# Reordered opening and turn, and idle TensorE instructions that fix where each visit stands in an instruction page

## The chip, the cores and the metric

The kernel runs on one core of one Trainium2 chip, as one launch. The metric is the device time of that core in microseconds (us), lower is better. TensorE multiplies matrices, VectorE (DVE), ScalarE (ACT) and GpSimd (POOL) do the rest of the arithmetic, SyncE (SP) issues transfers. Each engine has a sequencer that reads its own instruction stream in program order; engines wait for each other on semaphores.

## The reference, cut to what matters

Four attention modules follow each other. The change is in the first, L0, which has two cross-attention layers with 16 heads of width 128 over 32 sequences of 64 tokens, model width 256:

```python
def _cross_attention(q_in, kv_in, wq, bq, wk, bk, wv, bv, wo, bo, bias_k, bias_v):
    qh = (q_in @ wq + bq).reshape(b, q_len, H, K)      # H=16, K=128
    kh = (kv_in @ wk + bk).reshape(b, t, H, K)
    vh = (kv_in @ wv + bv).reshape(b, t, H, K)
    kh = concatenate([kh, bias_k]); vh = concatenate([vh, bias_v])
    weights = softmax(einsum('bqhk,bthk->bhqt', qh, kh) / sqrt(K))
    return einsum('bhqt,bthk->bqhk', weights, vh).reshape(b, q_len, H * K) @ wo + bo

x = x + _cross_attention(layer_norm(x), ctx, ...)       # layer 1
x = x + _cross_attention(layer_norm(x), ctx, ...)       # layer 2
x = x + gelu(layer_norm(x) @ w_fc1 + b_fc1) @ w_fc2 + b_fc2
```

After it come a perceiver attention, a decoder layer and a non-local block on the same data (the stretch from about 930 us on), which the change doesn't touch.

## The kernel before, in words

The 2,048 tokens are cut into 4 chunks (`NCH`) of 512 tokens. Heads are taken two at a time (a pair, with its own 1 MB pack of weights), so each layer has 8 pairs x 4 chunks = 32 steps `t`, and both layers together 64. Each of a step's products in float32 precision is three float32r matmuls (`split3`: high x high, high x low, low x high), all recorded at line 174.

TensorE's order is written out by hand. A block `d` handles the steps a = 2d and b = 2d+1. In an ordinary block (`pe_block`) TensorE does, in this order:

1. `pe_upper`: in every second pair of blocks first eight value tiles of the two steps before (`pe_values_behind`, 6 matmuls of 128x512 each); then four keys (`pe_key`, 6 matmuls of 128x512 each: two heads of a, two of b); two outputs (`pe_out`, 24 matmuls of 128x256 each); two transposes of probabilities.
2. `pe_queries`: four queries, 6 matmuls of 128x512 each.
3. `pe_visit`: probabilities times values of two earlier steps (`pe_heads`, L873, 128 records of matmuls and 128 of weight loads) and then the scores of a and b (`pe_scores`, L774, 64 and 64 records). A visit is 384 TensorE instructions, all tiny.

Four stretches are written separately: the opening (`pe_block_first`, `pe_block_second`: steps 0 to 3, with the layer norm of all chunks), the turn between the layers (`pe_block_turn`, `pe_block_after`: d = 16 and 17, with the layer norm of layer 2), the single steps at the end (`pe_singles`, steps 60 to 63), and the warm-up (16 matmuls on zeros, L1134, that wait for a memset). DVE, ACT and POOL have hand-written orders to match: `dve_attend`, `dve_block_turn`, `dve_block_after`, `act_attend`, `pool_attend`. Of these matter here: `dve_shift` (L1343, L1346: subtract the row's maximum from the scores; the next keys wait for it, since they reuse the scores' PSUM banks), `dve_values` (L1379, L1380: copy values out of PSUM), `context_dve` (L388: low part of the context), `norm0.dve_x` (L585: normalised rows), `norm0.dve_lo` (L602: low part of the normed rows, which queries wait for).

## Time and profile before

| | |
|---|---|
| median of 3 runs | 1558.56 us (1557.78 to 1559.69) |
| the profiled execution's own time | 1559.04 us |
| its span, first to last instruction | 1557.3 us |
| PE busy | 1505.2 us (97%) |
| DVE / ACT / POOL busy | 62% / 56% / 27% |
| mean granted TensorE clock | 0.993 |

The sum in the prediction is made against the profiled execution, 1559.04 us, which lies 0.5 us over the median. PE is matmuls, PEld weight loads, which overlap with matmuls. Waits are named by the instruction that ended last; "issue" means that the engine waited for nothing that the profile shows.

### The profile page before, as it was taken

What the parts mean: (1) busy time and instruction counts of PE and PEld (TensorE: products, weight loads), DVE (VectorE), ACT (ScalarE), POOL (GpSimd) and SP (SyncE); (2) the same over time, 40 slices, a digit from 0 to 9 for tenths busy, and PEclk for the clock granted to TensorE, in tenths of its full rate; (3) what the DMA queues carried; (4) which work ended last, traced back from release to release, by engine and by line L of the source; (5) the groups of instructions that cost most, each with busy time, mean ns of one, the idle gap of its engine ahead of it and who ended that gap; (6) DMA issues with size and microseconds to landing.
All of it is one profiled execution on the core that took longest, in us unless ns stands there. A gap on an engine that the chain in (4) does not pass through costs nothing. (4 is left out here: it accounts for less than half of the span.)

```text
span 1557.3 us, 41338 instructions
## 1 busy us (share of the span) xinstructions
PE 1505.2 (97%) x17264; PEld 1305.5 (84%) x17264; DVE 973.1 (62%) x2135; ACT 866.4 (56%) x1626; POOL 413.4 (27%) x445
## 2 busy tenths in 40 slices
PE   8899999999999999999999999999999999999996
PEld 7688888888888788888888888988878888888864
DVE  7746546554566664555646676479996558865366
ACT  5454353354455554454453466577777567775476
POOL 1320120210201510210210123036774206542052
PEclk9999999999999999999999999999999999999998
DMA  6010010010010010010010000020002000000001
GB/s 214 1 69 2 29 42 1 29 43 1 29 42 1 29 42 2 29 42 2 29 43 29 29 2 28 1 83 2 3 29 82 1 29 3 30 2 28 8 22 55
DMA packets 17832, 46.20 MB, mean 30 GB/s; under 512 B 1360, under 2 KB 11616, under 8 KB 14704
## 3 DMA queue, kind: packets, MB, share of 16 engines
q1 hardware_dynamic: 13456, 39.33, 7.3%
q10 hardware_dynamic: 4192, 4.24, 0.8%
q8 instruction: 137, 2.24, 0.6%
q14 instruction: 47, 0.39, 0.1%
HBM read 39.37 MB, written 4.19 MB: 28 GB/s over the span
## 5 line engine op out<-in xcount | busy, mean ns | idle before, releaser
L174 PE MATMUL ps<-ch,W 128*128 128x512 f32 (+1 forms) x2484 | 582.9, 384 | 12.7 <-DVE arena L1346 6.0
L174 PEld LDWEIGHTS ps<-ch,W 128*128 128x128 f32 x2484 | 437.8, 189 | 98.3 <-issue 5.9
L174 PEld LDWEIGHTS ps<-W,split_arena 128*128 128x128 f32 x3084 | 388.4, 188 | 23.5 <-issue 4.7
L174 PE MATMUL ps<-W,split_arena 128*128 128x256 f32 x3084 | 401.9, 283 | 3.4 <-DVE split_arena L1678 2.6
L1343 DVE TENSOR_REDUCE small<-ps 128x4 f32<-128x260 f32 x128 | 53.9, 421 | 241.3 <-PE ps L774 241.1
L1184 ACT ACTIVATE arena<-ps,hbias 128x512 f32<-128x512 f32 x128 | 87.9, 688 | 206.6 <-PE ps L174 205.6
L174 PE MATMUL ps<-W,ch 128*128 128x512 f32 (+1 forms) x864 | 193.7, 381 | 0.3
L1169 ACT ACTIVATE arena<-ps 64x256 f32<-64x256 f32 x256 | 96.8, 378 | 170.2 <-PE ps L860 166.4
L174 PEld LDWEIGHTS ps<-W,ch 128*128 128x128 f32 x864 | 154.6, 188 | 31.8 <-ACT arena L2166 0.9
L1678 DVE TENSOR_TENSOR split_arena<-arena,split_arena 128x512 fp32r<-128x512 f32 x96 | 72.1, 751 | 124.8 <-ACT split_arena L1710 115.0
L1370 DVE TENSOR_TENSOR x_sb<-ps,x_sb 128x512 f32<-128x512 f32 x128 | 87.0, 689 | 97.4 <-PE ps L174 97.2
L2440 POOL TENSOR_TENSOR arena<-arena,small 128x1024 f32<-128x1024 f32 x48 | 95.0, 1980 | 126.7 <-DVE small L2299 126.7
L1707 ACT ACTIVATE arena<-ps,cols 128x512 f32<-128x512 f32 x96 | 65.9, 687 | 92.5 <-PE ps L174 92.4
L219 POOL COPY hbias<-raw 128x8 f32<-128x8 f32 x15 | 3.3, 220 | 413.9 <-PE ps L174 413.9
L1191 ACT ACTIVATE arena<-ps,hbias 128x512 f32<-128x512 f32 x128 | 84.6, 686 | 35.9 <-PE ps L174 35.0
L1336 DVE SCALAR_TENSOR_TENSOR split_arena<-ps,hbias,split_arena 128x256 fp32r<-128x256 f32 x256 | 104.5, 475 | 0.0
L1176 ACT ACTIVATE split_arena<-ps,hbias 128x512 fp32r<-128x512 f32 x128 | 77.7, 687 | 14.0 <-PE ps L873 14.0
L613 POOL TENSOR_TENSOR small<-small 128x4 f32<-128x4 f32 x24 | 27.5, 1148 | 186.5 <-DVE small L486 172.7
L774 PE MATMUL ps<-arena 128*64 128x65 f32 x2048 | 69.7, 224 | 6.0 <-issue 5.9
L873 PEld LDWEIGHTS ps<-arena 64*64 64x64 f32 x4096 | 62.9, 135 | 13.2 <-issue 11.1
L1197 ACT ACTIVATE arena<-arena 128x260 f32<-128x260 f32 x128 | 52.4, 423 | 37.0 <-DVE arena L1346 37.0
L774 PEld LDWEIGHTS ps<-arena 128*64 128x64 f32 x2048 | 63.8, 138 | 10.1 <-issue 7.9
(172 smaller groups left out, 2020.4 us busy)
## 6 DMA issues: line engine op xcount, KB each, us to landing
raw<-wpack SPq DMA_DIRECT2D x23, 1028.0 KB, 4.8
rows<-vb_in SPq DMA_DIRECT2D x8, 512.0 KB, 5.7
x_sb<-x_in SPq DMA_DIRECT2D x4, 512.0 KB, 9.7
arena<-ctxT SPq DMA_DIRECT2D x4, 512.0 KB, 9.9
spill<-x_sb ACTq DMA_DIRECT2D x1, 2048.0 KB, 11.3
arena<-spill ACTq DMA_DIRECT2D x1, 2048.0 KB, 8.3
arena<-ctx_tok SPq DMA_DIRECT2D x16, 128.0 KB, 2.0
out<-x_sb SPq DMA_DIRECT2D x7, 256.0 KB, 2.5
```

Source lines behind the costliest of these rows:

```text
L174: last = e.matmul(dst, lhs[a], rhs[b], start=start and n == 0, stop=stop and n == 2, skip_group_check=True)
L774: ins = e.matmul(ps[r:r + SEQ, scores_bank(t) + h, n // 2 * KEYS0:(n // 2 + 1) * KEYS0], qs[t % 2][h][:, n * SEQ:(n + 1) * SEQ], ks[t % 2] ...
L873: ins = e.matmul(ps[dims, heads_bank(t) + b, at:at + SEQ], values[keys, h * DH0 + d * SEQ:h * DH0 + (d + 1) * SEQ], pts[t % 2][h][keys, n, ...
L1169: ins = e.activation(pts[t % 2][h][b * SEQ:(b + 1) * SEQ], own[:, :, b * SEQ:(b + 1) * SEQ], ACT.Copy)
L1176: e.activation(head_split(t, h, 0), head_cells(t, h), ACT.Identity, bias=head_col(t, 3, h)).then_inc(a_oh, 1)
L1184: e.activation(ks[u % 2][h][:, :, key_slots(h)], cut(ps[:, keys_bank(u) + h, :], BPC), ACT.Identity, bias=head_col(u, 1, h)).then_inc(a_ke, 1)
L1191: e.activation(qs[u % 2][h], ps[:, query_bank(u) + h, :], ACT.Identity, bias=head_col(u, 0, h)).then_inc(a_qe, 1)
L1336: ins = e.scalar_tensor_tensor(head_split(t, h, 1)[:, :, b, :], head_cells(t, h)[:, :, b, :], head_col(t, 3, h), head_split(t, h, 0)[:, :, ...
L1370: e.tensor_tensor(xs, cut(ps[:, b + j, :], 2), xs, ALU.add).then_inc(a_acc, 1)
L1678: e.tensor_tensor(gsp[f % 2][1], gelu[:, f % 2, :], gsp[f % 2][0].bitcast(F32), ALU.subtract).then_inc(s["gl"].sem, 1)
L1707: e.activation(gelu[:, f % 2, :], ps[:, f % 2, :], func, bias=col(f"fb{which}", f)).then_inc(s["gel"].sem, 1)
L2440: e.tensor_tensor(cells, cells, many(inv[w % 2], nk), ALU.mult).then_inc(nrm_done, 1)
```

## The change

It has four parts.

1. A new helper `idle(e, n)` puts n instructions on TensorE that only wait, for a semaphore (`none_ok`) that has been set since the first microseconds: 106 before the warm-up; 10 after each value tile of `pe_values_behind`; 24 after each key of a block whose number is a multiple of 4 (d = 4, 8, 12, 16, 20, 24, 28); 14 after six of the value tiles in `pe_block_after`. Four blocks then hold 2 x 80 + 96 = 256 of them.
2. Waits are moved out of the visits, onto earlier instructions (queries, outputs), so that a visit holds none.
3. Opening: low parts of context chunks 2 and 3 go from DVE to POOL (`context_lo`), the normalised rows of chunks 1 to 3 from DVE to ACT (`act_tiles`), and norms stand elsewhere in TensorE's order.
4. Turn and single steps: norms, value copies, low parts and POOL's powers are reordered; two PSUM bank choices follow.

```diff
@@ -548,7 +548,7 @@
             def act_tiles(self, e, c, l):
 
                 g = l * NCH + c
-                e.wait_ge(second_mean, c + 1)
+                e.wait_ge(second_mean, l * NCH + c)
                 e.wait_ge(self.s["T"].sem, self.s["T"].at(g * KT - 1))
                 for j in range(TPC):
                     ins = e.activation(xn[:, j, :], x_sb[:, c * TPC + j, :], ACT.Identity, scale=rstd[:, j:j + 1],
...
@@ -877,28 +876,38 @@
 
         none = sm[1].rearrange("p n k -> p (n k)")[:, 0:P]
 
+        PAGE_START, PAGE_TURN = 106, 14
+
+        def idle(e, n):
+
+            for _ in range(2 * n):
+                e.wait_ge(none_ok, 1)
+
         def pe_values_behind(e, d):
 
             a, b = 2 * d, 2 * d + 1
             for i in range(2):
                 e.wait_ge(a_sub, two(a, i))
                 pe_values(e, a, i)
+                idle(e, 10)
             for i in range(2):
                 e.wait_ge(a_sub, two(b, i))
                 pe_values(e, a, 2 + i)
+                idle(e, 10)
             e.wait_ge(a_ol, two(a - 2, 1))
             for i in range(2):
                 pe_values(e, b, i)
+                idle(e, 10)
             e.wait_ge(a_ol, two(b - 2, 1))
             for i in range(2):
                 pe_values(e, b, 2 + i)
+                idle(e, 10)
 
         def pe_visit(e, d):
 
             a, b = 2 * d, 2 * d + 1
             e.wait_ge(a_qe, two(a, 1))
             pe_heads(e, a - 2)
-            wait(e, a_acc, two(b - 4, 1))
             pe_heads(e, b - 2)
             pe_scores(e, a)
             pe_scores(e, b)
@@ -906,28 +915,32 @@
         def pe_upper(e, d):
 
             a, b = 2 * d, 2 * d + 1
-            behind = values_behind(d - 1)
-            if behind:
+            if values_behind(d - 1):
                 pe_values_behind(e, d - 1)
-            for h in range(2):
-                if behind:
+                for h in range(2):
                     e.wait_ge(a_ve, values_done(a - 2, h))
-                e.wait_ge(a_sub, two(a - 2, h))
-                pe_key(e, a, h)
-            for h in range(2):
-                if behind:
+                    pe_key(e, a, h)
+                for h in range(2):
                     e.wait_ge(a_ve, values_done(b - 2, h))
+                    pe_key(e, b, h)
+                pe_out(e, a - 4)
+                e.wait_ge(a_ve, values_done(b - 2, TPC - 1))
+                pe_out(e, b - 4, a)
+            else:
+                some = 24 if d % 4 == 0 else 0
+                for h in range(2):
+                    e.wait_ge(a_sub, two(a - 2, h))
+                    pe_key(e, a, h)
+                    idle(e, some)
                 e.wait_ge(a_ol, two(a - 4, 1))
-                pe_key(e, b, h)
-            if behind:
-                e.wait_ge(a_ve, values_done(a - 2, TPC - 1))
-            e.wait_ge(a_sub, two(b - 2, 1))
-            pe_out(e, a - 4)
-            if behind:
-                e.wait_ge(a_ve, values_done(b - 2, TPC - 1))
-            pe_out(e, b - 4)
+                for h in range(2):
+                    pe_key(e, b, h)
+                    idle(e, some)
+                e.wait_ge(a_sub, two(b - 2, 1))
+                pe_out(e, a - 4)
+                e.wait_ge(a_ol, two(b - 4, 1))
+                pe_out(e, b - 4, a)
             for i in range(2):
-                e.wait_ge(a_ke, two(a, i))
                 pe_transpose(e, a - 2 + i)
 
         def pe_queries(e, d):
...
@@ -960,19 +978,20 @@
             for h in range(2):
                 e.wait_ge(a_qe, two(0, h))
                 pe_key(e, 1, h)
-            e.wait_ge(a_ve, values_done(0, TPC - 1))
-            pe_norm(e, 0, 1)
             norm_out(e, 0, 0)
             for i in range(2):
                 pe_values(e, 1, i)
+            e.wait_ge(a_ve, values_done(0, TPC - 1))
+            pe_norm(e, 0, 1)
             for i in range(2):
                 e.wait_ge(a_ke, two(0, i))
                 pe_values(e, 1, 2 + i)
+            norm_out(e, 0, 1)
+            for h in range(2):
+                pe_query(e, 1, h)
             e.wait_ge(a_ke, two(1, 1))
             pe_norm(e, 0, 2)
-            norm_out(e, 0, 1)
-            for h in range(2):
-                pe_query(e, 1, h)
+            e.wait_ge(a_kb, 1)
             e.wait_ge(a_ve, values_done(1, TPC - 1))
             pe_scores(e, 0)
             pe_scores(e, 1)
...
@@ -1040,28 +1061,35 @@
             for i in range(2):
                 e.wait_ge(a_ke, two(b, i))
                 pe_values(e, a, i)
+                idle(e, PAGE_TURN)
             e.wait_ge(a_acc, two(a - 4, 1))
             for i in range(2):
                 pe_values(e, a, 2 + i)
+                idle(e, PAGE_TURN)
             e.wait_ge(a_pt, two(b - 2, 1))
             pe_norm(e, 1, 2)
             e.wait_ge(a_acc, two(b - 4, 1))
             pe_heads(e, a - 2)
             norm_out(e, 1, 2)
             pe_heads(e, b - 2)
-            for i in range(TPC):
+            for i in range(2):
                 e.wait_ge(a_ve, values_done(a, i))
                 pe_values(e, b, i)
+                idle(e, PAGE_TURN)
+            e.wait_ge(a_ve, values_done(a, TPC - 1))
+            pe_norm(e, 1, 3)
             e.wait_ge(a_ol, two(a - 2, 1))
-            pe_norm(e, 1, 3)
+            for i in range(2):
+                pe_values(e, b, 2 + i)
             for h in range(2):
                 e.wait_ge(a_ve, values_done(b, h))
                 pe_query(e, a, h)
-            for h in range(2):
-                e.wait_ge(a_ve, values_done(b, 2 + h))
+            norm_out(e, 1, 3)
+            for h in range(2):
                 pe_query(e, b, h)
             e.wait_ge(a_ol, two(b - 2, 1))
             pe_scores(e, a)
+            e.wait_ge(a_ve, values_done(b, TPC - 1))
             pe_scores(e, b)
 
         def pe_singles(e):
...
@@ -1143,18 +1184,21 @@
                     pe_block(e, d)
             pe_singles(e)
             next0.lead(e)
+            e.wait_ge(a_ol, two(STEPS - 2, 1))
             pe_out(e, STEPS - 2)
...
@@ -1233,16 +1277,19 @@
             act_keys(e, 0)
             act_norm(e, 0, 0)
             context_act(e, 1)
+            first_act(e, 4)
             act_queries(e, 0)
-            first_act(e, 4)
+            context_act(e, 2)
+            norm0.act_tiles(e, 1, 0)
             act_keys(e, 1)
             act_norm(e, 0, 1)
-            context_act(e, 2)
-            act_norm(e, 0, 2)
+            norm0.act_tiles(e, 2, 0)
             context_act(e, 3)
             act_queries(e, 1)
+            act_norm(e, 0, 2)
 
             act_exp(e, 0)
+            norm0.act_tiles(e, 3, 0)
             act_keys(e, 2)
             act_exp(e, 1)
...
@@ -1466,16 +1514,17 @@
             dve_mean(e, 1, 3)
             dve_values(e, a, (2, 3))
             dve_heads(e, a - 2)
+            dve_values(e, b, (0, 1))
             norm0.dve_lo(e, 2, 1)
+            norm0.dve_lo(e, 3, 1)
             dve_heads(e, b - 2)
-            dve_values(e, b)
-            norm0.dve_lo(e, 3, 1)
+            dve_values(e, b, (2, 3))
 
         def dve_attend(e):
             e.memset(minus_half, -0.5).then_inc(s_small.sem, 1)
             e.memset(none, 0.0).then_inc(none_ok, 1)
             dve_stats(e, 0, 0)
-            context_dve(e, 0)
+            context_lo(e, 0)
             first_dve(e, 0)
             norm0.dve_newton(e, 0)
             e.scalar_tensor_tensor(nmean, mv[:, :, 0], -1.0, rstd, ALU.mult, ALU.mult).then_inc(first_mean, 1)
@@ -1486,24 +1535,24 @@
                 first_dve(e, i)
             norm0.dve_lo(e, 0)
 
+            dve_values(e, 0, (0, 1))
+            context_lo(e, 1)
+            dve_stats(e, 0, 1)
+            dve_values(e, 0, (2, 3))
+            dve_mean(e, 0, 1)
             dve_bias_keys(e, 0)
-            dve_stats(e, 0, 1)
-            dve_values(e, 0)
-            context_dve(e, 1)
-            norm0.dve_x(e, 1)
             first_dve(e, 4)
             dve_stats(e, 0, 2)
+            dve_values(e, 1, (0,))
+            dve_mean(e, 0, 2)
             norm0.dve_lo(e, 1)
-            norm0.dve_x(e, 2)
-            dve_values(e, 1)
-            context_dve(e, 2)
+            dve_values(e, 1, (1, 2, 3))
             dve_stats(e, 0, 3)
+
+            dve_shifts(e, 0)
+            dve_mean(e, 0, 3)
+            dve_shifts(e, 1)
             norm0.dve_lo(e, 2)
-            norm0.dve_x(e, 3)
-            context_dve(e, 3)
-
-            dve_shifts(e, 0)
-            dve_shifts(e, 1)
             dve_scale(e, 0)
             dve_scale(e, 1)
             norm0.dve_lo(e, 3)
...
@@ -1570,7 +1619,10 @@
             e.tensor_copy(hbias[0], raw[:, PACK:PCOLS]).then_inc(hb_ok, 1)
             pair_bias(e, 0)
             norm0.pool_pow(e, 1)
+            e.wait_ge(c_lo.sem, c_lo.at(KT + KT - 1))
+            context_lo(e, 2)
             norm0.pool_pow(e, 2)
+            context_lo(e, 3)
             norm0.pool_pow(e, 3)
             e.wait_ge(s_raw, 16)
             pair_columns(e, 1)
@@ -1583,8 +1635,11 @@
                 split_pool(e, n, n - 2)
                 if n % 2:
                     split_half(e, n)
-            for c in range(NCH):
-                norm0.pool(e, c, row("bo2"), 1)
+            for c in (0, 2):
+                norm0.pool_pow(e, c, 1)
+                norm0.pool_pow(e, c + 1, 1)
+                norm0.pool_row(e, c, row("bo2"), 1)
+                norm0.pool_row(e, c + 1, row("bo2"), 1)
             for n in range(NHP + 1, 2 * NHP + 1):
                 split_pool(e, n, n - 2)
                 if n % 2 and n < NPAIR - 1:
```

The instructions that only wait are not listed in the orders below.

TensorE in the opening, from the first four value tiles to the first scores; before:

```order
L174 MATMUL ps<-W,ch 128x512 x24
L174 MATMUL ps<-ch,W 128x512 x24
L627 MATMUL ps<-cols,norm_arena 128x128 x8
L174 MATMUL ps<-W,ch 128x512 x24
L627 MATMUL ps<-cols,norm_arena 128x128 x8
L174 MATMUL ps<-ch,W 128x512 x12
L774 MATMUL ps<-arena 64x65 x32
```

and of the change:

```order
L174 MATMUL ps<-W,ch 128x512 x24
L174 MATMUL ps<-ch,W 128x512 x24
L174 MATMUL ps<-W,ch 128x512 x12
L627 MATMUL ps<-cols,norm_arena 128x128 x8
L174 MATMUL ps<-W,ch 128x512 x12
L174 MATMUL ps<-ch,W 128x512 x12
L627 MATMUL ps<-cols,norm_arena 128x128 x8
L773 MATMUL ps<-arena 64x65 x32
```

The two norms (L627, transposes) moved behind 12 more matmuls each; the scores stay last.

DVE just ahead of the first scores' maximum (L1343 before, L1390 now); before:

```order
L602 TENSOR_TENSOR ch<-norm_arena,ch 128x512 [waits n_hi] x2
L508 TENSOR_TENSOR small<-small 128x4 [waits n_pow,n_var]
L510 TENSOR_TENSOR small<-small 128x4 [waits n_r1]
L512 TENSOR_SCALAR small<-small 128x4 [waits n_r2]
L514 TENSOR_TENSOR small<-small 128x4 [waits n_r3]
L585 TENSOR_SCALAR norm_arena<-x_sb,small 128x256 [waits n_r4,n_T]
L585 TENSOR_SCALAR norm_arena<-x_sb,small 128x256 x3
L388 TENSOR_TENSOR ch<-arena,ch 128x512 [waits c_hi] x2
L1343 TENSOR_REDUCE small<-ps 128x4 [waits a_scores]
```

and of the change:

```order
L1426 TENSOR_TENSOR arena<-ps,arena 128x256 [waits a_values]
L1427 TENSOR_TENSOR arena<-ps,arena 128x256
L448 BN_STATS small<-x_sb 128x6 [waits s_x3,n_x]
L448 BN_STATS small<-x_sb 128x6 x3
L472 BN_AGGR small<-small 128x2 [waits n_st]
L472 BN_AGGR small<-small 128x2 x3
L486 TENSOR_SCALAR small<-small 128x4 [waits n_ag]
L1390 TENSOR_REDUCE small<-ps 128x4 [waits a_scores]
```

The low parts of chunk 2 (L602), the Newton steps and rows of chunk 3 (L508 to L585) and the context's low part (L388) no longer stand ahead of it; only copies of values and the statistics of chunk 3 do.

TensorE in `pe_block_after` (d = 17), from the norm of chunk 2 to the scores; before:

```order
L627 MATMUL ps<-cols,norm_arena 128x128 x8
L873 MATMUL ps<-arena 64x64 x64
L174 MATMUL ps<-W,ch 128x512 x24
L627 MATMUL ps<-cols,norm_arena 128x128 x8
L174 MATMUL ps<-ch,W 128x512 x24
L774 MATMUL ps<-arena 64x65 x32
```

and of the change:

```order
L627 MATMUL ps<-cols,norm_arena 128x128 x8
L872 MATMUL ps<-arena 64x64 x64
L174 MATMUL ps<-W,ch 128x512 x12
L627 MATMUL ps<-cols,norm_arena 128x128 x8
L174 MATMUL ps<-W,ch 128x512 x12
L174 MATMUL ps<-ch,W 128x512 x24
L773 MATMUL ps<-arena 64x65 x32
```

The norm of chunk 3 (second L627) now stands between the value tiles of step b, not behind them.

## Rows read from the trace of the kernel before

**Rows 1.** The page's head: the span, busy time of each engine, instruction fetches.

```profile
span 1557.3 us, 41338 instructions
PE 1505.2 (97%) x17264; PEld 1305.5 (84%) x17264; DVE 973.1 (62%) x2135; ACT 866.4 (56%) x1626; POOL 413.4 (27%) x445
...
q8 instruction: 137, 2.24, 0.6%
```

**Rows 2.** Waits of TensorE, 0 to 930 us: us in total, times, longest.

```profile
PE ps L174 <- DVE arena L1346: 6.0, 2, 5.5
PE ps L774 <- issue: 5.9, 9, 1.8
PE ps L174 <- DVE arena L1380: 3.1, 2, 1.6
...
PE ps L627 <- DVE arena L1380: 2.2, 1, 2.2
PE ps L174 <- DVE ch L602: 1.7, 2, 0.9
```

**Rows 3.** TensorE in order of time, two visits: start, us, work, [idle before].

```profile
92.98 2.09 PE L873 MATMUL ps<-arena 64*64 64x64 f32 x128
95.01 2.08 PE L774 MATMUL ps<-arena 128*64 128x65 f32 x64
97.02 5.79 PE L174 MATMUL ps<-ch,W 128*128 128x512 f32 x24
...
114.85 2.09 PE L873 MATMUL ps<-arena 64*64 64x64 f32 x128
...
118.97 0.81 PE L774 MATMUL ps<-arena 128*64 128x65 f32 x20 [0.58 <-issue]
119.71 5.79 PE L174 MATMUL ps<-ch,W 128*128 128x512 f32 x24
```

**Rows 4.** The last visit with such a stop, same columns.

```profile
766.87 2.09 PE L873 MATMUL ps<-arena 64*64 64x64 f32 x128
...
771.47 2.81 PE L174 MATMUL ps<-ch,W 128*128 128x512 f32 x11
```

**Rows 5.** Waiting instructions by line: duration ns min/median/max, first to last start us.

```profile
L864 PEldq EVENT_SEMAPHORE  x1: 51/51/51, 56.5 to 56.5; - x1
L865 PEldq EVENT_SEMAPHORE  x1: 2263/2263/2263, 56.6 to 56.6; - x1
L865 PEldq EVENT_SEMAPHORE  x1: 51/51/51, 110.7 to 110.7; - x1
L2755 DVEq EVENT_SEMAPHORE  x13: 21/21/21, 0.8 to 1.9; - x13
...
L2755 PEldq EVENT_SEMAPHORE  x3: 51/51/51, 0.8 to 1.1; - x3
```

**Rows 6.** TensorE in order of time, the opening.

```profile
2.28 5.69 PE L1134 MATMUL ps<-arena 128*128 128x128 f32 x32 [2.28 <-DVE arena L1476]
8.27 1.20 PE L811 MATMUL ps<-ch,W 128*128 128x512 f32 x4 [0.29 <-ACT W L276]
...
43.77 7.32 PE L174 MATMUL ps<-ch,W 128*128 128x512 f32 x24 [5.46 <-DVE arena L1346]
...
59.33 2.10 PE L873 MATMUL ps<-arena 64*64 64x64 f32 x128
...
64.30 11.22 PE L174 MATMUL ps<-W,ch 128*128 128x512 f32 x48
```

**Rows 7.** TensorE in order of time, the turn.

```profile
476.42 1.22 PE L627 MATMUL ps<-cols,norm_arena 128*128 128x128 f32 x8 [2.18 <-DVE arena L1380]
477.29 7.29 PE L174 MATMUL ps<-ch,W 128*128 128x512 f32 x24
...
517.86 3.01 PE L174 MATMUL ps<-ch,W 128*128 128x512 f32 x12 [1.60 <-DVE arena L1380]
521.76 3.00 PE L174 MATMUL ps<-ch,W 128*128 128x512 f32 x12 [0.89 <-DVE ch L602]
```

100 lines of the change are left out of this document (61 added, 39 removed).

## The prediction, on record before the changed kernel ran

> **What bounds the kernel now.** I read the page first, then the waits of TensorE, then its timeline. TensorE (PE) is busy 97% of the span and no other engine passes 62% [rows 1], so a microsecond counts only where PE stops. Up to 930 us, the stage that is changed, its stops are few [rows 2]: the first scores' shift (L1346, 5.5 us at once), value copies (L1380), low parts (L602), and nine stops of 5.9 us together inside the scores (L774) that end by "issue": no engine is late.
>
> Those nine come at a fixed place. An undisturbed visit lasts from 92.98 to 97.02, 4.04 us; the visit at 114.85 lasts until 119.71, 4.86 us, and PE stands still after 44 of its 64 scores records [rows 3]. The stream holds 34,528 weight loads and matmuls [rows 1] and 705 waiting instructions, and is fetched in 137 pieces [rows 1]: 257 each, so I take a page as 256. Counting the built program from the stop in the visit at 59.33 to that at 118.97 gives 1,256 loads and matmuls plus 24 waits, 1,280 = 5 pages; every other stop also lies a whole number of pages away. In instructions from a visit's first one to the next page start, the visits that stop stand at 45 to 134 (45, 68, 86, 93, 118, 134), the others at 3, 20, 38, 163, 183, 205 and more. So a stop needs two page starts inside, or just at the end of, one visit's 384 quick instructions: the second page isn't there yet. The last such visit takes 4.60 us [rows 4], the first 4.97 [rows 6]; eleven visits are over 4.04 us by 9.2 us in all (first 0.93, last 0.56).
>
> The skill is cited once on this: the Trainium skill, "Runtime: NRT & Kernel Launch", section on instruction fetch mechanics, has blocks of 256 instructions, as counted here, but says that crossing a boundary is mostly hidden. The trace disagrees for visits (0.58 us [rows 3]); by that rule the new places would give back nothing and the sum below would be 8.1 us higher.
>
> **The change part by part.**
>
> *Places of the visits: -8.1 us.* Counted in the built program, the distances to the next page start become 14, 14, 14, 190, repeating, both in the safe sets. So 9.2 us go. New risks: the visit in the turn stands at 137 and a single-step visit at 59 with its second page start 7 instructions before the end. I book the turn's below and 1.1 us for the single one, between the smallest stop I see and the longest, 1.8 [rows 2].
>
> *What an idle instruction costs: 0.11 us of PE's sequencer.* The trace shows no long run of them on PE, so this is bounded. Its record lasts 51 ns [rows 5]: the lower end. Two adjacent ones, L864 and L865, start at 56.5 and 56.6 [rows 5], 0.1 us apart; a run of three on PE, which also set a semaphore, starts 0.8 to 1.1, 0.15 apart: the upper end. That a run costs start to start, not by its records, is shown on DVE: 13 with 21 ns records take from 0.8 to 1.9, 0.09 each. I take 0.11, nearest to the pair.
>
> *What covers it.* The sequencer runs ahead of the engine. The wait ahead of the visit (L865) is done at 110.7 and the visit starts at 114.85 [rows 3, 5]: 4.15 us at 0.234 us a matmul (11.22/48 [rows 6]) is about 18 matmuls, 35 instructions. At the end of a visit these 35 are scores, 2.01 us for 128 instructions [rows 3], only 0.55 us of work.
>
> *24 after each key, seven blocks: +32.9 us.* A key is 6 matmuls, 1.41 us. The keys come straight after a visit. When the first key's 12 instructions are issued, 23 scores instructions (0.36 us) and the key (1.41) are ahead: 1.77 us. 24 idles take 2.64 us, so PE stops about 0.9 us (0.05 to start again). Now nothing is ahead: after each of the other three keys it stops 2.64 - 1.41 + 0.03 = 1.26 us. That is 0.92 + 3 x 1.26 = 4.7 us a block, and d = 4, 8, 12, 16, 20, 24, 28 make 32.9. Behind the idles stand outputs, transposes and queries; no other engine gives the time back, because PE has no stops of theirs to spare there. What PE does later in the block (outputs, so DVE's additions) is late by as much.
>
> The Trainium skill ("TensorE: Matmul & The Clock Gate", facts table) gives the engine's queue 64 places; the trace shows 35. By 64 the first stop of each block would shrink by at most 29 scores instructions, 0.46 us, and the sum by 3.2 us.
>
> *10 after each value tile: 0.* 1.1 us against 1.41 us of matmuls; the cover grows with each. Without cover it would still be free. *14 in the block after the turn: +0.* 1.54 against 1.41, 0.13 short each, which the 0.55 us or more ahead covers.
>
> *106 at the start: +11.3 us.* The first one waits for the memset, as the warm-up does now (2.28 [rows 6]). 106 x 0.11 = 11.7, so the warm-up runs from 13.9 and, at 5.7 us, ends at 19.6; the first keys start at 8.27 now. The loads and first splits that they wait for are then long done.
>
> *Opening, given back: -9.3, new waits +0.5.* With PE 11.3 us late and DVE not, what PE waited for is there: 5.46 at the first keys of block 1, and with it the slow clock behind it (24 matmuls in 7.32 us [rows 6] against 5.79 [rows 3]: 1.5), 1.5 of L1380 (3.1 less the turn's 1.6 [rows 2, 7]), 0.8 of L602 (1.7 - 0.9). The reordering helps too: between scores and shift DVE has only copies and one set of statistics left. POOL gets two low parts and three powers in line; a power behind them can hold a norm, hence the 0.5. Opening together: 11.3 - 9.3 + 0.5 = +2.5.
>
> *Turn: -3.3 us.* The norm of chunk 1 waits 2.18 us for the sixth value copy [rows 7]. The low part that stood among the copies still stands there, but statistics and Newton steps now overlap POOL's power: 0.8 less. Of the slow clock behind it (7.29 against 5.79) I count half, 0.8. In the block after, queries waited 1.60 and 0.89 [rows 7] for copies and a low part that now come earlier; the norm that is pulled forward may wait 0.6 for ACT's rows: -1.9. A visit there gains a page stop of 0.5 and another loses 0.3: +0.2.
>
> Single steps: waits change places, 0 +-1. Later stages: same code, other places in the page, and none of their stops shows this pattern, 0 +-1.
>
> **Sum.** 1559.0 + 32.9 (24s) + 2.5 (opening) - 3.3 (turn) - 8.1 (pages) = **1583.0 us** for a profiled execution, and 1582.6 against the median; I say 1583.
>
> **The rivals.**
>
> *Idles cost their record, 51 ns; the kernel gets faster.* For it: the record. Against it: rows 5, where no engine starts the next waiting instruction when the record of the last ends. Then 24 take 1.22 us, under the key's 1.41, and nothing stops. The start costs 5.4 instead of 11.7, so keys start 5.1 us later and, being less late, still wait 1.5 us of the 9.3: 5.1 - 9.3 + 1.5 = -2.7. 1559.0 - 2.7 - 3.3 - 8.1 = 1545. It turns at about 0.075 us an idle: then three stops of 0.42 and one of 0.1 in seven blocks make 9.5 us and the start costs 8. Chance 0.11, and 0.02 for landing on the turning point (within 0.2% of before, which is about what a measurement tells from no change).
>
> *The clock falls in the 24s.* PE then works 1.41 and rests 1.26 us, four times. It fell to 1.2 GHz (granted 0.5) after 2.18 us of rest in the turn, not after the 1.8 us stop [rows 2, 7]; each fall costs 1.5 us (7.29 against 5.79). One fall in each of seven blocks: 1583 + 10.5 = 1593. Chance 0.12.
>
> *Places don't matter:* something else in the visits stops PE and the 9.2 us stay: 1591. Against it, the whole pages between stops. Chance 0.05.
>
> *Idles at 0.15,* as in the run of three: 24 take 3.6, a block stops 0.96 more four times, seven blocks 27, the start 4: 1583 + 31 = 1614. They also set a semaphore there, the new ones don't. Chance 0.04.
>
> The forecast itself has 0.66.
>
> **How the numbers follow.** 1583 is the forecast's; its own range is 1573 to 1592: 0.01 us on an idle moves it 8 us (24 x 4 x 7 x 0.01 and the start), opening and turn 3 each. The range for 8 in 10 takes in the clock and the places: 1566 to 1598; outside lie the faster rival, 0.15 and a little more. Faster 0.11, same 0.02, slower 0.87.
>
> **What would show it.** In the changed profile: the first keys at about 19.6 us; in blocks 4, 8, ... four stops by "issue" ahead of L174, one near 0.9 and three near 1.26 us; waiting instructions 0.11 us apart; all ordinary visits 4.04 us, no issue stop in the scores save one in the single steps; no 5 us stop at 40 us; the norm in the turn waiting 1.4 us or less. It is wrong if idles lie 0.05 to 0.07 us apart, for then the 24s vanish under the keys, or if a stopped PE loses its clock each time.

## The result and the profile after

The changed kernel takes 1591.76 us (median of 4 runs, 1589.39 to 1592.99) against 1559.12 us (1557.78 to 1560.3) for the kernel before beside it: ratio 1.0205, 95% interval 1.0189 to 1.0221. The forecast was 1583, its range 1566 to 1598. The profiled execution of the change took 1591.85 us, 32.8 more than that of before; its span is 32.8 us longer too. Below, a "stop" is a stretch in which PE stands still between two matmuls, and "the 24s" are the 24 idle instructions behind each key.

The head of the page, which answers to [rows 1]:

```profile
span 1590.1 us, 42905 instructions
...
PE 1509.6 (95%) x17264; PEld 1302.6 (82%) x17264; DVE 972.4 (61%) x2122; ACT 874.3 (55%) x1638; POOL 419.1 (26%) x449
...
q8 instruction: 143, 2.34, 0.6%
```

PE does the same 17,264 matmuls in nearly the same busy time (4 us more); nearly all of the loss is standing still. The waits of PE up to 930 us, us in total, times, longest, which answer to [rows 2]:

```profile
PE ps L174 <- issue: 19.1, 21, 1.2
PE ps L1175 <- issue: 13.7, 1, 13.7
PE ps L174 <- DVE split_arena L1383: 7.8, 7, 1.2
PE ps L627 <- DVE arena L1427: 3.0, 1, 3.0
PE ps L627 <- ACT norm_arena L554: 2.0, 1, 2.0
PE ps L773 <- issue: 1.3, 3, 0.7
```

L174 has 21 + 7 = 28 stops: four in each of the seven blocks with 24 idles. (Those put down to L1383 are such stops too; block 4 below has one.) The 5.5 us stop of before [rows 2] is gone and a 13.7 us one stands at the start; the page stops in the scores went from nine to three.

PE in order of time, in four stretches: opening, visit and block 4, turn, block behind the turn (start, us, work, [idle before]). It answers to [rows 3, 6, 7].

```profile
13.72 6.66 PE L1175 MATMUL ps<-arena 128*128 128x128 f32 x32 [13.72 <-issue]
20.14 1.17 PE L811 MATMUL ps<-ch,W 128*128 128x512 f32 x4
...
49.70 5.75 PE L174 MATMUL ps<-ch,W 128*128 128x512 f32 x24
...
63.64 2.10 PE L872 MATMUL ps<-arena 64*64 64x64 f32 x128
...
66.80 1.85 PE L773 MATMUL ps<-arena 128*64 128x65 f32 x56 [0.69 <-issue]
68.58 1.67 PE L174 MATMUL ps<-W,ch 128*128 128x512 f32 x6
...
119.18 2.10 PE L872 MATMUL ps<-arena 64*64 64x64 f32 x128
...
123.22 1.67 PE L174 MATMUL ps<-ch,W 128*128 128x512 f32 x6
125.58 1.61 PE L174 MATMUL ps<-ch,W 128*128 128x512 f32 x6 [0.69 <-issue]
128.18 1.60 PE L174 MATMUL ps<-ch,W 128*128 128x512 f32 x6 [0.99 <-DVE split_arena L1383]
130.95 1.63 PE L174 MATMUL ps<-ch,W 128*128 128x512 f32 x6 [1.17 <-issue]
133.60 6.00 PE L174 MATMUL ps<-W,split_arena 128*128 128x256 f32 x48 [1.02 <-issue]
...
497.60 1.97 PE L627 MATMUL ps<-cols,norm_arena 128*128 128x128 f32 x8 [3.01 <-DVE arena L1427]
...
535.94 1.06 PE L627 MATMUL ps<-cols,norm_arena 128*128 128x128 f32 x8 [1.99 <-ACT norm_arena L554]
```

- The first keys start at 20.14 (8.27 before [rows 6]). From 68.58 on the ordinary blocks run; before, they began at 64.30 [rows 6]: +4.3 us, with the first visit as long as before, 4.94 us here.
- The visit at 119.18 ends at 123.22: 4.04 us, no stop. Of 28 full visits 26 are so, where before it was 17; only the first (63.64) and the last, at 875.75 (4.60 us), are longer.
- Block 4 stops four times: once by 0.69 and then by about 1 us of idle time. From start to start, less a key's 1.41, the four are 0.95, 1.19, 1.36 and 1.24 us, where 0.92 and three of 1.26 were forecast. From the visit ahead of it to the next (at 145.86) it takes 26.68 us; such a block without idles takes 21.87. That is 4.8 us a block and 33.8 in seven.
- In the turn the norm waits 3.01 us, not 2.18 [rows 7], and another norm waits 1.99. From the visit ahead of the turn (461.39) to the first ordinary one behind (566.25) it is 104.86 us, 4.83 of them the idles; before it was 98.66 (445.85 to 544.51): +1.4.

The idles themselves, those of the start, of which 105 are recorded: duration ns min/median/max, first to last start in us:

```profile
L884 PEldq EVENT_SEMAPHORE  x105: 51/51/51, 2.3 to 13.5; - x105
```

Start to start that is 11.2/104 = 0.108 us, with records of 51 ns. The first idle behind the first key of block 4 starts at 122.89, 0.33 us ahead of that key (123.22); the forecast had 0.36, from a sequencer 35 instructions ahead.

Where 32.7 us went, from the starts of the last visit (923.83 before, 956.52 after), in the forecast's own terms:

| term | forecast | measured |
|---|---|---|
| 24 idles, seven blocks | +32.9 | +33.8 |
| opening to the first ordinary block | +2.5 | +4.3 |
| turn | -3.3 | +1.4 |
| visits' places, with the single steps and the rest | -8.1 | -7.6 + 0.8 |
| sum | +24.0 | +32.7 |

Of the 0.8, 0.25 lies in the single steps (75.92 us from the end of the last full visit to the start of the last visit before, 76.17 after). The other 0.6 lies in blocks behind visits that no longer stop: before, such a block was up to 0.18 us shorter than 17.83, so a part of the stop came back.

So the one large term held, and two of the terms I built on waits, opening and turn, did not; the turn has the wrong sign. The experiments take the terms one at a time.

### The profile page after: what moved, and what is told of

Its sections match the earlier page's. It is cut to its first block and busy times, and to the rows that moved or that the text cites. A ratio compares the mean times of both kernels' runs of the same rounds, so it can differ in the third digit from the quotient of the medians.

```text
span 1590.1 us, 42905 instructions
## 1 busy us (share of the span) xinstructions
PE 1509.6 (95%) x17264; PEld 1302.6 (82%) x17264; DVE 972.4 (61%) x2122; ACT 874.3 (55%) x1638; POOL 419.1 (26%) x449
## 5 line engine op out<-in xcount | busy, mean ns | idle before, releaser
L174 PE MATMUL ps<-ch,W 128*128 128x512 f32 (+1 forms) x2484 | 585.9, 384 | 22.9 <-issue 11.8
L174 PEld LDWEIGHTS ps<-ch,W 128*128 128x128 f32 x2484 | 434.6, 188 | 114.8 <-issue 32.2
L174 PEld LDWEIGHTS ps<-W,split_arena 128*128 128x128 f32 x3084 | 388.0, 188 | 32.4 <-issue 14.7
L174 PE MATMUL ps<-W,split_arena 128*128 128x256 f32 x3084 | 402.3, 283 | 10.7 <-issue 7.6
L1390 DVE TENSOR_REDUCE small<-ps 128x4 f32<-128x260 f32 x128 | 53.8, 420 | 234.2 <-PE ps L773 234.1
L174 PE MATMUL ps<-W,ch 128*128 128x512 f32 (+1 forms) x864 | 194.2, 382 | 0.3
L174 PEld LDWEIGHTS ps<-W,ch 128*128 128x128 f32 x864 | 154.4, 188 | 31.8 <-ACT arena L2221 0.9
L1383 DVE SCALAR_TENSOR_TENSOR split_arena<-ps,hbias,split_arena 128x256 fp32r<-128x256 f32 x256 | 104.4, 474 | 0.0
L1220 ACT ACTIVATE split_arena<-ps,hbias 128x512 fp32r<-128x512 f32 x128 | 78.0, 688 | 13.2 <-PE ps L872 13.0
L872 PEld LDWEIGHTS ps<-arena 64*64 64x64 f32 x4096 | 63.1, 135 | 13.2 <-issue 11.6
L2378 DVE TENSOR_REDUCE small<-ps 128x8 f32<-128x1024 f32 (+1 forms) x48 | 58.4, 1217 | 18.4 <-PE ps L2124 18.0
L872 PE MATMUL ps<-arena 64*64 64x64 f32 x4096 | 68.0, 220 | 1.3 <-ACT arena L1235 0.8
L773 PE MATMUL ps<-arena 128*64 128x65 f32 x2048 | 67.9, 223 | 1.3 <-issue 1.3
```

The lines of the kernel that those rows point to most:

```text
L174: last = e.matmul(dst, lhs[a], rhs[b], start=start and n == 0, stop=stop and n == 2, skip_group_check=True)
L773: ins = e.matmul(ps[r:r + SEQ, scores_bank(t) + h, n // 2 * KEYS0:(n // 2 + 1) * KEYS0], qs[t % 2][h][:, n * SEQ:(n + 1) * SEQ], ks[t % 2] ...
L872: ins = e.matmul(ps[dims, heads_bank(t) + b, at:at + SEQ], values[keys, h * DH0 + d * SEQ:h * DH0 + (d + 1) * SEQ], pts[t % 2][h][keys, n, ...
L1220: e.activation(head_split(t, h, 0), head_cells(t, h), ACT.Identity, bias=head_col(t, 3, h)).then_inc(a_oh, 1)
L1383: ins = e.scalar_tensor_tensor(head_split(t, h, 1)[:, :, b, :], head_cells(t, h)[:, :, b, :], head_col(t, 3, h), head_split(t, h, 0)[:, :, ...
```

## The experiments

Times are medians, and the ratio is to the kernel before on the same chip, with its 95% interval. Differences between versions are of medians, which came from different chips in part; the kernel before lay between 1559.1 and 1559.7 us on them. "The turn" is the time from the start of the visit ahead of it to that of the first ordinary visit behind it; "over 4.04" is what the 28 full visits take above 4.04 us each.

### Without the 24s

```diff
-                some = 24 if d % 4 == 0 else 0
+                some = 0
```

> The changed kernel without the 24 idles after each key (7 blocks, 672 instructions less); the other idles stay. Theory A (an idle costs TensorE's sequencer 0.11 us and the 24s outlast the key ahead of them): 7 x 4.83 us go, but the visits no longer stand at one place; counted in the program, nine visits stand at 46 to 118 from the next page start and one at 126, which by the stops of the kernel before is 8.6 us; 1591.8 - 33.8 + 8.6 - 0.9 = 1565.7. Rival B (the loss comes from the waits that were moved out of the visits and the idles are free): about 1592 plus page stops, 1600.

Measured: 1565.31 us, 1.0036 (1.0024 to 1.0048), as theory A has it. The 24s cost 26.5 us net: 33.8 from the stops, less what the places give, since without them the visits drift through the page and are 9.9 us over 4.04 again.

### No idle at all, the order of the change

```diff
-            for _ in range(2 * n):
-                e.wait_ge(none_ok, 1)
+            return
```

> The changed kernel with every idle left out: the reordered opening and turn alone. Theory A: 24s gone (-33.8), page stops come back (six visits at 120, four at 44, two at 124: +12), and the start is 11.9 us earlier of which the opening's own waits take back 5 to 8: 1591.8 - 33.8 + 12 - 5.5 = about 1564. The opening ends (start of the third block) between 61 and 65 us against 64.3 before and 68.6 in the changed kernel. Rival B: 1590 or more.

Measured: 1558.06 us, 0.9991 (0.9982 to 1.0). I expected 1564, with the ordinary blocks from 61 to 65 us. The ordinary blocks start at 56.56 us, where before it was 64.30 [rows 6]: the new order of the opening alone gives 7.7 us, and TensorE was not late at all in this run (first keys at 7.90). The visits are 13.2 over 4.04, the turn takes 100.6.

### The kernel before with only the 24s

```diff
                 pe_key(e, a, h)
+                idle(e, 24 if d % 4 == 0 else 0)
```

> The kernel before with the 24 idles after each key of blocks 4, 8, ... 28 and nothing else of the change. Theory A: +33.8, and page stops change from 9.2 to about 5.6 us since the visits move: 1559.1 + 33.8 - 3.6 = 1589.3, with four stops in each of seven blocks. Rival B (idles free): 1556.

Measured: 1593.19 us, 1.0210 (1.0194 to 1.0225), 4 us over the expectation. The 24s cost about the same in the old order: the keys of block 4, with their stops, take 10.3 us (119.52 to 129.84) and 10.4 in the change (123.22 to 133.60). What I missed is the visits, which at their shifted places were 9.6 over 4.04, not 5.6. A stop at a given distance comes back, but not with the same length (0.1 to 1.7 us in this run).

### The same idles, spread

The four blocks keep 256 idles, but never more than 8 in one spot outside `pe_values_behind` (10) and the block behind the turn (14): behind keys, behind each half of the outputs, behind queries, and in the turn behind value tiles in place of queries. The edit in part:

```diff
-                some = 24 if d % 4 == 0 else 0
+                some = 8 if d % 4 == 0 else 0
...
+                    idle(e, some // 2)
```

> The changed kernel with the same 96 idles in each of the seven blocks, at most 8 in one place: 8 after each of four keys, 4 after each quarter of the two outputs, 8 after each of four queries (in the turn: four value tiles). Every visit stands at the same place in its page as in the changed kernel. Theory A (an idle is free while its run is shorter than the matmuls ahead of it: 0.88 against 1.41 us, 0.44 against 0.72): 1591.8 - 33.8 = 1558.0, and no stop in those blocks. Rival C (each idle costs time wherever it stands): no change, 1592.

Measured: 1558.26 us, 0.9991 (0.9982 to 1.0). The same number of idles costs nothing when none of the runs outlasts the work in front of it: 33.5 us lie between this kernel and the change. Block 4 in it, PE in order of time:

```profile
122.88 5.79 PE L174 MATMUL ps<-ch,W 128*128 128x512 f32 x24
128.50 5.92 PE L174 MATMUL ps<-W,split_arena 128*128 128x256 f32 x48
```

The 24 matmuls of the keys run through in 5.6 us, which took 10.4 with the 24s.

### Runs of seven lengths

```diff
-                some = 24 if d % 4 == 0 else 0
+                some = {4: 12, 8: 14, 12: 16, 16: 18, 20: 20, 24: 22, 28: 28}.get(d, 0)
```

> The change with 12, 14, 16, 18, 20, 22 and 28 idles behind each key in blocks 4, 8, 12, 16, 20, 24 and 28, in place of 24 in each. It measures the price of an idle inside the kernel. My theory, 0.11 us an idle and hidden up to the 1.41 us of a key: no stop at 12, nearly none at 14 (0.1 or less each), and per block about 1.1, 2.0, 2.9, 3.8 and 6.5 us for 16, 18, 20, 22 and 28 idles. Rival (a fixed price for any run of idles, such as a restart of the queue): the blocks with 12 and 14 stop too, and 28 costs hardly more than 16. The visits leave their common place, so some of them stop in a page again.

Measured: 1581.72 us, 1.0141 (1.0126 to 1.0157). From the end of a visit to the start of the next a block without idles takes 17.83 us; with four runs of 12, 14, 16, 20, 22 and 28 idles it took 0, 0.3, 1.2, 2.8, 3.7 and 6.3 us more (block 16 is the turn and is left out). I had expected 1.1, 2.9, 3.8 and 6.5 for the last four. From 20 to 28 that is 3.5 us for 32 idles, 0.11 each; the price starts between 12 and 14, where 0.11 x 13 equals a key's 1.41. No fixed price shows. Keys of block 28 in it (28 idles each):

```profile
814.14 1.63 PE L174 MATMUL ps<-ch,W 128*128 128x512 f32 x6 [1.08 <-DVE arena L1393]
817.21 1.63 PE L174 MATMUL ps<-ch,W 128*128 128x512 f32 x6 [1.44 <-issue]
820.25 1.63 PE L174 MATMUL ps<-ch,W 128*128 128x512 f32 x6 [1.42 <-issue]
```

From 814.14 to 817.21 are 3.07 us, 28 x 0.11: the key lies wholly beneath its idles.

### The kernel before with only the 106 at the start

```diff
         def pe_attend(e):
+            for _ in range(2 * 106):
+                e.wait_ge(none_ok, 1)
             e.wait_ge(none_ok, 1)
```

> The kernel before with only the 106 idles at the start. My theory: the warm-up and the first keys come 11.9 us later (first keys at 20.1 us), the stops that follow in the old opening (5.5 at the first keys of block 1 with its slow clock, copies and low parts, 9.3 us together) are given back because the other engines are not late, so block 2 starts 2.6 us later than before, at about 66.9 us; the visits stand at other places, of which some 9 again stop, so they give nothing. Together 1561 to 1563 us. Rival (the other engines' work is itself tied to TensorE, so the stops are not given back): block 2 starts 8 to 12 us later, 1567 to 1571 us.

Measured: 1568.07 us, 1.0063 (1.0049 to 1.0077). My theory fell here: the ordinary blocks start at 74.27 us, 10.0 later than before, as the rival has it. The stop that I had "given back" stands where it was. PE in order of time, then DVE:

```profile
18.75 1.17 PE L811 MATMUL ps<-ch,W 128*128 128x512 f32 x4
...
53.31 7.83 PE L174 MATMUL ps<-ch,W 128*128 128x512 f32 x24 [5.45 <-DVE arena L1348]
```

```profile
37.95 1.29 DVE L602 TENSOR_TENSOR ch<-norm_arena,ch 128x512 fp32r<-128x512 f32 x2 [0.49 <-ACT ch L651]
...
47.27 1.29 DVE L602 TENSOR_TENSOR ch<-norm_arena,ch 128x512 fp32r<-128x512 f32 x2
...
49.87 1.38 DVE L585 TENSOR_SCALAR norm_arena<-x_sb,small 128x256 f32<-128x256 f32 x4 [0.18 <-DVE small L514]
51.17 1.28 DVE L388 TENSOR_TENSOR ch<-arena,ch 128x512 fp32r<-128x512 f32 x2
52.37 0.42 DVE L1345 TENSOR_REDUCE small<-ps 128x4 f32<-128x260 f32 x1
```

The stop is 5.45 us long, against 5.46 [rows 6], although PE is 10.5 us late (18.75 against 8.27). DVE reaches the maximum (L1345) only after low parts, value copies, statistics, Newton steps, rows and a context part, almost back to back from 37.95 on (0.7 us of waits in 14.4). The first of these (L602, 37.95) itself waited for ACT's high part (L651), which is made of PE's transposes. In the kernel before the same DVE operation starts at 28.40, 9.55 us earlier: DVE had moved back with PE.

### The start's 106 idles spread over the opening

On top of the spread version: 5 or 6 idles behind each of the 21 groups of 6 matmuls in the two opening blocks, none before the warm-up. All visits from the first full one on keep their places. The edit in part:

```diff
+        opening = iter([PAGE_START // groups + (n < PAGE_START % groups) for n in range(groups)])
+        def few(e):
+            idle(e, next(opening, 0))
...
+                few(e)
...
-            idle(e, PAGE_START)
```

> The change with its 256 idles a four-block spread (at most 8 in one place), and now also the 106 idles of the start taken from before the warm-up and laid 5 at a time behind the groups of 6 matmuls of the two opening blocks, so that each run hides under 1.4 us of matmuls. All visits stand at the same places of a page as with the 106 at the start. My theory (an idle costs 0.11 us of TensorE's sequencer and is free under cover; the 106 pay 11.7 us before any work is there): the start of block 2 comes at 56.6 to 57.5 us instead of 67.9, and the kernel takes about 1547 us. Rival (the reordered opening is bound by DVE and ACT, so that the early start only moves the wait): start of block 2 at 61 or later and 1551 to 1553 us.

Measured: 1546.37 us, 0.9917 (0.9904 to 0.9931), 11.9 us faster than with the 106 in front. PE in order of time:

```profile
8.80 1.17 PE L811 MATMUL ps<-ch,W 128*128 128x512 f32 x4
...
38.37 5.75 PE L174 MATMUL ps<-ch,W 128*128 128x512 f32 x24
...
57.24 3.01 PE L174 MATMUL ps<-W,ch 128*128 128x512 f32 x12
```

There is no 5.5 us stop behind the scores although the first keys start at 8.80: the order removes it, lateness does not. The ordinary blocks start at 57.24, 10.7 us earlier than with the 106 in front (67.89). Another 1.5 us is in the turn (98.5 against 100.05), where the granted clock fell to 0.5 in the profiled execution of the spread version (behind a stop of 2.90 us) and stayed at 1.00 in this one (behind 2.87). That is in part luck of the execution: the mean clock of the eleven runs of the spread version, one kernel, lies between 0.993 and 0.997.

### POOL's order in the turn as before

```diff
-            for c in (0, 2):
-                norm0.pool_pow(e, c, 1)
-                norm0.pool_pow(e, c + 1, 1)
-                norm0.pool_row(e, c, row("bo2"), 1)
-                norm0.pool_row(e, c + 1, row("bo2"), 1)
+            for c in range(NCH):
+                norm0.pool(e, c, row("bo2"), 1)
```

On top of the spread version. The reason for it is in the trace of the change: DVE (two stretches) and then POOL, in order of time:

```profile
485.46 0.16 DVE L514 TENSOR_TENSOR small<-small 128x4 f32<-128x4 f32 x1
...
491.41 0.62 DVE L508 TENSOR_TENSOR small<-small 128x4 f32<-128x4 f32 x1
492.06 0.66 DVE L510 TENSOR_TENSOR small<-small 128x4 f32<-128x4 f32 x1
492.76 0.67 DVE L512 TENSOR_SCALAR small<-small 128x4 f32<-128x4 f32 x1
493.46 0.65 DVE L514 TENSOR_TENSOR small<-small 128x4 f32<-128x4 f32 x1
494.15 0.16 DVE L1439 SCALAR_TENSOR_TENSOR small<-small 128x4 f32<-128x4 f32 x1
```

```profile
490.29 1.01 POOL L613 TENSOR_TENSOR small<-small 128x4 f32<-128x4 f32 x1 [5.93 <-DVE small L486]
491.27 2.83 POOL L409 TENSOR_TENSOR x_sb<-x_sb,rows 128x256 f32<-128x256 f32 x4
```

While POOL adds rows (491.27 to 494.10), each of DVE's four Newton steps takes 0.62 to 0.67 us; at 485.46, without POOL beside it, a step of the same shape takes 0.16, and so does L1439 just after the rows. With POOL's powers put ahead of the rows, DVE gets the power early and meets the rows.

> The change with spread idles, and POOL's order in the turn as it was before (for each chunk first its powers, then its row additions) in place of powers of two chunks and then rows of two chunks. My theory (the turn lost because POOL's row additions now run while DVE does its Newton steps on 128x4, which take 0.62 to 0.70 us instead of 0.16 and delay value copies and rows of chunk 3): DVE's Newton steps come back to about 0.16 us, the turn from visit 15 to visit 19 takes 97 to 98.5 us instead of 100.05, and the kernel 1555 to 1557 us. Rival (the loss comes from TensorE's own new order in the turn): the Newton steps get shorter and the turn stays at 100.

Measured: 1553.24 us, 0.9963 (0.995 to 0.9977), 5.0 us faster than with the change's POOL order. The same step of DVE, then PE's norm, in this run:

```profile
473.12 0.16 DVE L514 TENSOR_TENSOR small<-small 128x4 f32<-128x4 f32 x1
```

```profile
476.76 1.09 PE L627 MATMUL ps<-cols,norm_arena 128*128 128x128 f32 x8 [1.44 <-DVE arena L1433]
...
513.14 1.06 PE L627 MATMUL ps<-cols,norm_arena 128*128 128x128 f32 x8 [0.92 <-ACT norm_arena L554]
```

The turn takes 95.39 us, better than the 97 to 98.5 I gave: both norms wait less (1.44 and 0.92 against 2.90 and 1.6 in the spread version), and the granted clock doesn't fall behind the first.

### The kernel before with the change's POOL order

The reverse edit, in the kernel before:

```diff
-            for c in range(NCH):
-                norm0.pool(e, c, row("bo2"), 1)
+            for c in (0, 2):
+                norm0.pool_pow(e, c, 1)
...
+                norm0.pool_row(e, c + 1, row("bo2"), 1)
```

> The kernel before with one edit: POOL's order in the turn as in the change (powers of chunks 0 and 1, then the row additions of both; the same for 2 and 3). My theory (the row additions, 0.75 us each, hold up VectorE's small operations with two operands in SBUF): VectorE's Newton steps of chunk 1 take 0.6 to 0.7 us instead of 0.16, the stop of 2.18 us at the norm in the turn grows to 4 to 4.5 us, chunk 3 loses less, and the kernel is 2 to 4.5 us slower, 1561.5 to 1564 us. Rival (POOL's order only hurts in TensorE's new order): within 1 us of before.

Measured: 1563.96 us, 1.0021 (1.0012 to 1.0030), so some 3.3 us slower (4.6 by the medians), by the ratio within the 2 to 4.5 expected; the stop at the norm grew to 3.62 us, less than the 4 to 4.5 expected. DVE, then PE, in order of time:

```profile
471.78 0.66 DVE L510 TENSOR_TENSOR small<-small 128x4 f32<-128x4 f32 x1
```

```profile
477.95 1.97 PE L627 MATMUL ps<-cols,norm_arena 128*128 128x128 f32 x8 [3.62 <-DVE arena L1380]
```

The slow Newton steps appear here too, in the old order of TensorE and DVE; the turn takes 102.8 us instead of 98.66. POOL's order is the cause in both.

### Both remedies

The edits of the last two versions of the change in one kernel:

```diff
-            idle(e, PAGE_START)
...
+                few(e)
...
+            for c in range(NCH):
+                norm0.pool(e, c, row("bo2"), 1)
```

> The two edits that helped, together: the idles of the start spread over the opening blocks and POOL's order in the turn as before, with the spread 256 idles a four-block. If they are independent (one acts before 57 us, the other in the turn), the turn from visit 15 to visit 19 takes 95.4 us and the kernel 1546.4 - 4.9 = 1541.5 us (1540.5 to 1542.5). Rival (the turn's gain depends on where the opening left the other engines or on transfers that come at another moment): 1543 or more.

Measured: 1542.83 us, 0.9891 (0.9875 to 0.9906). The turn takes 95.0. The median lies 1.3 us over the expected sum and just under the rival's 1543; the profiled execution took 1541.48, so the runs don't decide between the two. One thing would make the sum too large: the 1.5 us that the first edit's profile gained in the turn, by the kept clock, are in the second edit's gain too.

### Other places

On top of both remedies:

```diff
-        PAGE_START, PAGE_TURN = 106, 14
+        PAGE_START, PAGE_TURN = 136, 14
...
-                some = 8 if d % 4 == 0 else 0
+                some = 8 if d % 4 == 0 and d != TURN or d == TURN + 1 else 0
```

> As the version with both edits, but 136 instead of 106 idles in the opening and 64 of the turn block's idles moved to the block behind it, so that the visits stand 240 or 160 instructions before the next page start instead of 14 or 190, and the turn's visit at 171. My theory (a stop needs the second page start inside a visit with the sequencer's lead used up; at 14 it comes 112 instructions before the visit's end and is marginal: stops of 0.3 to 0.6 us remained in 5 visits and 0.9 in the first; at 240 and 160 only one page start lies inside the visit's quick part and is preceded by slow instructions): no stop in any ordinary visit but small ones, the sum over 4.04 us falls from 3.1 to under 0.7 us, and the kernel is 2 to 3 us faster than the version with both edits alone, 1538.5 to 1540 us. Rival (14 was as good as any place and the remaining stops come from transfers that delay the fetch): same time within 1 us.

Measured: 1542.45 us, 0.989 (0.9873 to 0.9906): the same, as the rival has it. My theory was right only on the visits. All full visits but the first take 4.04 us, so 240 and 160 are cleaner places than 14; but in the version with both remedies the visits behind the first, at 14 and 190, were only 1.0 over. The first visit stops more, by 1.30 us and among its heads, behind 242 instructions, where the first page start stands at 243, and the block behind the turn, where the 64 idles went, takes 0.9 more. The first visit's stop:

```profile
52.61 2.02 PE L874 MATMUL ps<-arena 64*64 64x64 f32 x121
55.93 0.34 PE L874 MATMUL ps<-arena 64*64 64x64 f32 x7 [1.30 <-issue]
```

### The reordering alone, with POOL's old order

The version without any idle, and:

```diff
+            for c in range(NCH):
+                norm0.pool(e, c, row("bo2"), 1)
```

> No idle instruction at all, the reordered opening, turn and single steps, and POOL's order in the turn as before: what the reordering alone gives without the visits' places. The version without idles took 1558.06; with POOL's order the turn gives 4.7 back, so 1553.4 us (1552.5 to 1554.5); visits stop at their unplanned places by 10 to 13 us in total. Against the version with both edits the difference, about 12 us, is what places are worth. Rival: places worth only 9 us, the stops of the kernel before; then 1550.5.

Measured: 1553.13 us, 0.9954 (0.994 to 0.9968). Its visits are 14.0 over 4.04; in the version with both remedies it was 1.9. The places are worth 10.3 us in time (12.1 in the visits' own lengths). PE's waits, first row:

```profile
PE ps L773 <- issue: 9.7, 14, 1.5
```

## Why the prediction was right and wrong

- **The 24s: right.** 4.7 us a block forecast, 4.8 measured; four stops, one smaller (0.95 from start to start for 0.92), as worked out. With 64 instructions ahead in place of 35 the first would have been 0.46. The price (0.108 us start to start, not the 51 ns record) and the cover (a key, and 0.55 us once) are shown by the blocks with 12 to 28 idles, and the spread version shows that the number of idles doesn't matter, only each run's length.
- **The rivals.** "Idles cost their record" fell with the 0.108 us. "The clock falls in the 24s" fell: the granted clock stayed at 1.0 through all seven blocks. "Places don't matter" fell: 26 of 28 visits are undisturbed. Here the rule of the Trainium skill ("Runtime: NRT & Kernel Launch", instruction fetch mechanics), that crossing a boundary is mostly hidden, holds for most of the 137 page starts, but not for those in the visits: 10.3 us hang on the places. Its block of 256 agrees: the profile's page shows 6 more fetches (143 for 137 [rows 1]) for 1,567 more instructions, 1,559 of them TensorE's.
- **The opening: the number near (+2.5 for +4.3), the step wrong.** The step that failed is "with PE 11.3 us late and DVE not, what PE waited for is there". The kernel before with only the 106 shows 0.5 us given back of 9.3 (10.5 late at the first keys, 10.0 at the ordinary blocks): DVE's work before the scores' maximum hangs on PE's output, so it is as late as PE. What did remove the stop and its slow clock is the new order, 7.7 us without any lateness, a cause I booked as a mere help. That the total came near is luck: two misses met, a lateness that is not given back and an order worth 7.7. The start cost what I said: the ordinary blocks begin at 67.9 with the 106 in front and at 56.56 without, 11.3 apart (0.45 of it a longer stop in the first visit), and 11.3 - 7.7 = 3.6. The profiled run of the change lies 0.7 above that, because its warm-up took 6.66 us and that of the version without 24s, with the same opening, 5.95.
- **The turn: wrong sign, the largest miss (4.7 us).** The step that failed is "statistics and Newton steps now overlap POOL's power: 0.8 less". They do, but POOL's row additions then fall on the Newton steps, which take four times as long, and the norm waits 3.01 us for the copies behind them. I had priced POOL's new order by who waits for whom, not by what runs side by side. With POOL's old order the turn takes 95.39 against 98.66 us, -3.27: the gain forecast for TensorE's and DVE's new order is there, and the powers' order costs 4.7. That it is -3.27 for -3.3 is luck in part: the clock is kept whole (6.62 us from the norm to the visit for 8.09, where I counted half), and the visit's heads stop by 0.46. The SBUF page of the Trainium skill ("SBUF — State Buffer", two separate sides) states that a VectorE operation with two inputs in SBUF and a GpSimd operation that reads SBUF, or one in a two-port mode and any GpSimd operation, exclude each other for a whole instruction. The traces agree: a row addition takes 0.71 us (2.83/4), a Newton step beside it 0.62 to 0.67, while copies out of PSUM beside such additions stay at 0.41 (476.30 in the version with POOL's old order). Whether the step at L512, which has one tensor as input and takes 0.67 too, ran in a two-port mode isn't shown here.
- **The places: right in kind,** -7.6 us where 9.2 was the most (the eleven visits add up to 9.1). Two stops that I had counted as gone stayed: the first visit's, 0.90 over at 17 instructions ahead of a page start, and the last full visit's, 0.56 over at 14, which is not as safe a place as I took it for. The single steps cost 0.25, where I had booked 1.1.

The account of the places can be tested on all 14 kernels together: visits' places counted in the built programs as in the prediction, stops and fetches read from the traces.

- Where a visit stops: without the first visits of each kernel, 158 full visits stand 137 to 254 instructions ahead of a page start, and none stops. Of 95 at 44 to 134, 92 stop; of 125 nearer than 44, 23.
- Where in it: PE's 96 stops inside full visits all begin at a page start, 0 to 6 instructions ahead of it (the visits of before hold 5 waits, which I don't count here).
- What ends it: each of the 96 ends 1.1 to 1.6 us after a fetch of the instruction queue has landed.
- Why two page starts are too many: no two of the 1,967 fetches start closer than 3.25 us, while a visit gets through 256 instructions in 2.7 us (4.04 x 256/384).

So the missing page is shown by place and time. That two fetches can't follow closer for a reason of their own was not tested. In the change's first visit they lie 3.5 us apart (16 slices of the row below); the GB/s row over 60 to 69 us, 40 slices of 0.225:

```profile
GB/s 0 0 0 0 0 0 0 0 0 0 0 0 0 0 0 0 0 0 0 73 0 0 0 0 0 0 0 0 0 0 0 0 0 0 0 73 0 0 0 0
```

Why a stop at one place has different lengths (in visits 120 instructions ahead, 0.1 to 1.0 us) is open in part. Transfers into the core play a role that I overlooked. Where SyncE's loads (weight packs, mostly) run in the 3 us ahead of a visit and into it, a visit at 44 to 134 is 1.15 us over 4.04 in the mean of 36; where none does, 0.59 in the mean of 59. Nearer than 44, all 7 visits with such a load stop, and 16 of 118 without. The change's last full visit is one of the 7; a load of 1028 KB runs until 876.5:

```profile
877.77 0.45 PE L773 MATMUL ps<-arena 128*64 128x65 f32 x7
878.51 1.90 PE L773 MATMUL ps<-arena 128*64 128x65 f32 x57 [0.29 <-issue]
```

Its fetch starts 0.33 us behind the visit's start; in the undisturbed visits at the same place, 14, it starts 0.1 to 1.8 us ahead of it. In the five kernels with their last full visit at 14 it stops by 0.56 to 0.65 us. At 240, with the same load, it doesn't. This is read from runs made for other ends: no run moves a load and nothing else. Why the first visit stops at every place it was given (118, 123, 17, 12, 243 instructions ahead of a page start), without a load, stays open.

## What to carry to other kernels

Padding of an instruction stream is free as long as each piece is shorter than the work queued in front of it, and beyond that costs what it is longer by (four runs of 28 idles behind keys of 1.41 us: 6.3 us; of 12: nothing): spread it, and never put it before the first work. Before you book a stop as "given back" because one engine starts later, follow what the other engine does before the release: if that hangs on the late engine's output, the stop moves along with it. When a reordering lets two engines start together, look at what they will run side by side, and not only at the waits.

## What the runs showed of the hardware that was not expected

- An instruction that only waits, on a semaphore long set, takes TensorE's sequencer 0.108 us, twice its record of 51 ns.
- VectorE's 128x4 operations on SBUF take 0.62 to 0.67 us instead of 0.16 while GpSimd adds rows.
- The granted clock fell to 0.5 (1.2 GHz) behind stops of 2.18, 2.90 and 3.01 us in the turn and not behind one of 2.87, each in one profiled execution, and stayed up behind four stops of 0.7 to 1.4 us in a row.
- Fetches of TensorE's instructions start at least 3.25 us apart (1,967 of them), and a stop ends 1.1 to 1.6 us after one has landed.
- Stops are about twice as long where a load of SyncE's runs into the visit (1.15 us for 0.59 in the mean, 95 visits), and nearer than 44 instructions to a page start all 7 visits with a load stop, 16 of 118 without.
- Two page starts within a visit cost 0.4 to 2.0 us, in 11 visits 9.1 us in total before; the best version found, with spread idles and POOL's old order, is at 0.989 of the kernel before.
